# Query projection and output projection of a gated cross-attention kernel as three matmuls of high and low parts

## The reference

```python
# layer 1 (the code calls it L0): 16 heads of 16
q  = LN_head(LN(x) @ Wq)                 # per head layer norm of queries and keys
k, v = ctx @ Wkv
x  = x + tanh(g0) * (softmax(q k^T) v @ Wp + bp)      # Wp: the output projection of layer 1
x  = x + tanh(f0) * tanh(LN(x) @ W @ aux1 @ aux2 + b)
# layer 2 (L1): 8 heads of 64, keys from the tokens too
x  = x + tanh(g1) * (softmax(q1 [k1; k2]^T) [v1; v2] @ Wo + bo)
x  = x + tanh(f1) * mixture_of_8_experts(LN(x))       # the 2 best of 8 for each token
```

## Time and profile before

| | |
|---|---|
| median of 3 runs | 584.75 us (584.33 to 585.51) |
| the profiled execution, first to last instruction | 581.6 us |
| PE busy | 555.4 us, 95% |
| weight loads (PEld), beside PE | 477.1 us, 82% |
| DVE busy | 408.8 us, 70% |
| ACT busy | 319.4 us, 55% |
| POOL busy | 271.9 us, 47% |
| layer 1's quads | about 19 to 202 us |

### The profile page before, as it was taken

How to read it: one execution, slowest core, us unless ns; L and a number is a source line. 1 busy time by engine, 2 the same in 40 slices (tenths; PEclk the granted TensorE clock), 3 DMA queues, 4 the chain that set the end, 5 groups by cost and what they waited for, 6 DMA issues and landing times.

```text
span 581.6 us, 13614 instructions
## 1 busy us (share of the span) xinstructions
PE 555.4 (95%) x5542; PEld 477.1 (82%) x5542; DVE 408.8 (70%) x831; ACT 319.4 (55%) x632; POOL 271.9 (47%) x237
## 2 busy tenths in 40 slices
PE   8999999999989999999999999998999999999994
PEld 8776667677657878888888888877899999979994
DVE  7877568578696666777767867767677677746652
ACT  3554555555664665566555556654465656636641
POOL 3755655765740164657567465731203233421424
PEclk9999999999999999999999999999999999999998
DMA  8910840000000000000000000019374567726112
GB/s 259 357 45 2 318 194 3 1 3 2 2 2 1 2 1 2 8 9 17 18 9 18 10 25 1 25 26 414 91 253 149 170 213 253 259 32 236 28 20 26
DMA packets 24091, 50.92 MB, mean 88 GB/s; under 512 B 7072, under 2 KB 17104, under 8 KB 20688
## 3 DMA queue, kind: packets, MB, share of 16 engines
q1 hardware_dynamic: 18560, 45.20, 21.4%
q0 software_dynamic: 4224, 3.70, 3.6%
q10 hardware_dynamic: 1232, 1.01, 0.6%
HBM read 37.89 MB, written 13.31 MB: 88 GB/s over the span
## 4 chain that ended last, share of the span: by engine, by line
PE 81%; DVE 7%; ACT 5%; POOL 4%; issue 2%; DMA 1%; POOLq 0%; DVEq 0%; ACTq 0%
PE ps L59 15%; PE ps L60 14%; PE ps L61 14%; PE ps L607 5%; PE ps L750 4%; PE ps L625 4%; PE ps L768 4%; PE ps L738 4%; ACT P L1642 3%; DVE KN L1140 3%; PE ps L641 3%; PE ps L515 2%; PE ps L816 2%; POOL P L1947 2%; PE ps L522 2%
## 5 line engine op out<-in xcount | busy, mean ns | idle before, releaser
L1947 POOL TENSOR_SCALAR P<-P,rinv 112x487 f32<-112x487 f32 x56 | 88.2, 1588 | 50.9 <-DVE rinv L1183 50.7
L1140 DVE TENSOR_REDUCE KN<-ps 112x4 f32<-112x1500 f32 x32 | 55.0, 1719 | 28.7 <-PE ps L607 28.6
L424 POOL DMA_INDIRECT out<-WS,rows_i x16 | 28.7, 1791 | 92.5 <-ACT WS L1789 89.0
L60 PE MATMUL ps<-XGf,WH 128*128 128x256 f32 x252 | 71.3, 283 | 0.0
L61 PE MATMUL ps<-XGf,WL 128*128 128x256 f32 x252 | 71.3, 283 | 0.0
L59 PE MATMUL ps<-XGf,WH 128*128 128x256 f32 x252 | 71.3, 283 | 0.0
L1886 POOL TENSOR_TENSOR sr<-sv,mhalf 125x32 f32<-125x32 f32 x13 | 70.7, 5435 | 1.1
L1521 DVE TENSOR_TENSOR WL<-WR,WH 128x1024 fp32r<-128x1024 f32 x48 | 57.1, 1219 | 13.6 <-ACT WH L1843 10.0
L1642 ACT ACTIVATE P<-ps 125x1344 f32<-125x1344 f32 x32 | 41.3, 1292 | 32.8 <-PE ps L625 32.8
L1705 ACT ACTIVATE P<-ps,nm 112x487 f32<-112x487 f32 x64 | 41.9, 664 | 31.7 <-DVE nm L1175 31.7
L1843 ACT ACTIVATE WH<-WR 128x1024 fp32r<-128x1024 f32 x48 | 48.7, 1049 | 0.1
(11 more groups left out here) (290 smaller groups left out, 1546.1 us busy)
## 6 DMA issues: line engine op xcount, KB each, us to landing
WR<-in_gupT SPq DMA_DIRECT2D x16, 1024.0 KB, 7.2
WR<-in_dwnT SPq DMA_DIRECT2D x8, 1024.0 KB, 10.3
xs<-ZT SPq DMA_DIRECT2D x14, 516.0 KB, 6.0
CT<-in_ctxT SPq DMA_DIRECT2D x1, 2250.0 KB, 11.1
P<-xs SPq DMA_DIRECT2D x7, 256.0 KB, 10.8
P<-xs SPq DMA_DIRECT2D x9, 128.0 KB, 2.6
Wk<-in_L_xattn_Wk SPq DMA_DIRECT2D x2, 512.0 KB, 11.1
Wv<-in_L_xattn_Wv SPq DMA_DIRECT2D x2, 512.0 KB, 11.1
```

Source lines behind the costliest of these rows:

```text
L60: e.matmul(out, ah, bl, start=False, stop=False)
L1140: e.tensor_reduce(heads(KN[b % 2][0:NQ, 3, :])[:, 4 * k:4 * k + 4, 16], ps[0:NQ, 0:4, 0:NC], AX.X, ALU.max, negate=True).then_inc(s("smax" ...
L1947: e.tensor_scalar(P[:, k, 0:487], P[:, k, 0:487], rinv[:, k:k + 1], None, ALU.mult).then_inc(s("psc"), 1)
```

## The change

Two projections of layer 1 are computed by `matmul3` in place of float32 matmuls: the query projection of batches 3 to 7 (`QUERY_SPLIT = 3`), and the output projection of all 8 batches.

- The weights `Wp` and `Wq0` are split once, by new steps `wd 0` and `wd 1`: the high part on ACT (128x512), the low part on DVE (128x512).
- For batches 3 to 7, `xtc b 0` writes the high part of the turned tokens, and a new step `xtl b 0` on DVE computes the low part (128x224). It reads PSUM too, so that the bank of `xt b 0` is read out by `xtl`, no longer by `xtc`.
- `aT` of layer 1 writes the high part, and a new step `aTl` on DVE the low part (128x224). The bank of `awT` is read out by `aTl`.
- `WO` is loaded by SP after the eighth `wo` and behind the DMAs from `ZT`, no longer at the start. Its place in SBUF now holds `DH`, the high parts of `Wp` and `Wq0`, until then.

```diff
+QUERY_SPLIT = 3
...
+def has_low(b, r):
+
+    return r == 0 and b >= QUERY_SPLIT
...
+    if stage == "xt" and has_low(*i):
+        return ("xtl", *i)
+    if stage == "awT":
+        return ("aTl", *i)
...
-PREP = ((-38.14, "cs"), (-46.29, "norm", 0), (-31.45, "kp", 1, 0), (-31.42, "xt", 0), (-31.79, "xtc", 0),
+PREP = ((-38.14, "cs"), (-46.29, "norm", 0), (-31.45, "kp", 1, 0), (-31.42, "xt", 0), (-31.79, "xtc", 0), (-31.2, "xtl", 0),
...
                         for sem_, v in emptied(("xt", b, 0)):
                             w.wait_ge(sem_, v)
+                        if b >= QUERY_SPLIT:
+                            w.wait_ge(s("wd"), dense_split(1))
                         for k in range(2):
-                            t = e.matmul(ps[0:NQ, bk, 256:512], XT[:, k, b * NQ:(b + 1) * NQ], Wq0[:, k, :],
-                                         start=(k == 0), stop=(k == 1))
+                            if b < QUERY_SPLIT:
+                                t = e.matmul(ps[0:NQ, bk, 256:512], XT[:, k, b * NQ:(b + 1) * NQ], Wq0[:, k, :],
+                                             start=(k == 0), stop=(k == 1))
+                            else:
+                                t = matmul3(e, ps[0:NQ, bk, 256:512], tokens(b, k), [W_[:, k, :] for W_ in Wqs],
+                                            k == 0, k == 1)
...
+                        elif n < NB:
+                            t = matmul3(e, ps[0:NQ, bk, 0:256], [a[:, g * NQ:(g + 1) * NQ] for a in aT0],
+                                        [W_[:, g, :] for W_ in Wps], g == 0, g == nt - 1)
...
+                elif stage == "xtl":
+                    b, r = i
+                    w.wait_ge(s("xth"), high_order.index((b, r)) + 1)
+                    if b > QUERY_SPLIT:
+                        w.wait_ge(s("kp"), o_("kq", b - 1, 0))
+                    e.tensor_tensor(XTl, ps[:, bank("xt", b, r), 0:2 * NQ].rearrange("p (k n) -> p k n", k=2),
+                                    f_(XTh[:, :, b * NQ:(b + 1) * NQ]), ALU.subtract).then_inc(bank_sem("xt", b, r), 1)
+                elif stage == "aTl":
+                    n, = i
+                    if n:
+                        w.wait_ge(s("wo"), n)
+                    w.wait_ge(s("aT0"), n + 1)
+                    e.tensor_tensor(aT0[1], ps[:, bank("awT", n), 0:2 * NQ], f_(aT0[0]),
+                                    ALU.subtract).then_inc(bank_sem("awT", n), 1)
+                elif stage == "wd":
+                    k, = i
+                    w.wait_ge(s("wda"), dense_split(k))
...
+                    (high, low), W = ((Wps, Wp), (Wqs, Wq0))[k]
+                    e.tensor_tensor(low, W, f_(high), ALU.subtract).then_inc(s("wd"), 1)
...
-            e.dma_start(WO, pk("L1_xattn_Wo")).then_inc(s("in_WO"), 16)
...
+            w.wait_ge(s("wo"), NB)
+            e.dma_start(WO, A["L1_xattn_Wo"].rearrange("(k p) n -> p k n", p=128)).then_inc(s("in_WO"), 16)
```

More of the change, by code:

```diff
@@ L115 @@
 VALUES_1 = ((-15.23, "v", 1, 0), (-15.6, "vc", 1), (0.74, "v", 0, 0), (3.95, "v", 0, 1), (5.45, "vc", 0))
-TAIL0 = ((27.84, "ob"), (30.99, "obT"), (31.7, "aw"), (33.53, "awT"), (34.16, "aT"), (45.83, "wo"),
+TAIL0 = ((27.84, "ob"), (30.99, "obT"), (31.7, "aw"), (33.53, "awT"), (34.16, "aT"), (34.9, "aTl"), (45.83, "wo"),
          (47.46, "res", 1), (58.84, "stats", 1), (64.34, "norm", 1), (71.13, "xt", 1), (72.21, "xtc", 1),
@@ L191, in attention_order @@
         for d, stage, *i in (PREP if b >= 2 else ()) + (VALUES if b >= 2 else VALUES_1 if b else ()) + TAIL0:
-            at(t + d, stage, b, *i)
+            if stage != "xtl" or has_low(b, *i):
+                at(t + d, stage, b, *i)
     for d, stage in FFW:
@@ L352, in build @@
         FW = [cols(2048 + 512 * i, 2, 256) for i in range(3)]
+        XTh = XTo[:, :].rearrange("p (a b) -> p a b", a=2)
+        XTl = tile("XTl", 128, 2, NQ)
+        Wqs, Wps = ([t.rearrange("p (a b) -> p a b", a=2) for t in (B["DH"][:, 512 * k:512 * k + 512], XGf[:, o:o + 512])]
+                    for k, o in enumerate((0, 1536)))
         GW = sb("GW", [128, 2, NE])
@@ L527, in context0, with tokens, dense_split @@
             return t
+        def tokens(b, k):
+            return XTh[:, k, b * NQ:(b + 1) * NQ], XTl[:, k, :]
+        dense_order = [x[1] for x in order.entries if x[0] == "wd"]
+        def dense_split(k):
+            return dense_order.index(k) + 1
+        high_order = [x[1:] for x in order.entries if x[0] == "xtc" and has_low(*x[1:])]
         def tensor_attention(e, w):
@@ L801, in tensor_attention @@
                     bk = take(stage, n)
-                    nt, W = (2, Wp) if n < NB else (4, WO)
-                    w.wait_ge(s("in_Wp" if n < NB else "in_WO"), 16)
+                    nt = 2 if n < NB else 4
+                    if n >= NB:
+                        w.wait_ge(s("in_WO"), 16)
                     if n < NB:
+                        w.wait_ge(s("wd"), dense_split(0))
                         for sem_, v in emptied(("awT", n)):
@@ L1071, in vector_attention @@
                                     ALU.subtract).then_inc(s("cs"), 1)
+                elif stage == "xtl":
[15 more added lines that the diff above has]
+                    w.wait_ge(s("wda"), dense_split(k))
+                    if k:
+                        for b in range(QUERY_SPLIT):
+                            w.wait_ge(s("kp"), o_("kq", b, 0))
+                    (high, low), W = ((Wps, Wp), (Wqs, Wq0))[k]
+                    e.tensor_tensor(low, W, f_(high), ALU.subtract).then_inc(s("wd"), 1)
                 elif stage == "xs1":
@@ L1542, in scalar_attention @@
                     w.wait_ge(s("xt"), o_("xt", b, r))
-                    e.activation(XT[:, :, b * NQ:(b + 1) * NQ],
+                    low = has_low(b, r)
+                    e.activation((XTh if low else XT)[:, :, b * NQ:(b + 1) * NQ],
                                  ps[:, bank("xt", b, r), 0:2 * NQ].rearrange("p (k n) -> p k n", k=2),
-                                 ACT.Copy).then_inc(bank_sem("xt", b, r), 1)
+                                 ACT.Copy).then_inc(s("xth") if low else bank_sem("xt", b, r), 1)
                     if r == 3:
@@ L1650, in scalar_attention @@
                                  ACT.Copy).then_inc(bank_sem(src), 1)
+                elif stage == "wd":
+                    k, = i
+                    if k:
+                        w.wait_ge(s("dve0"), Q_SET)
+                    else:
+                        w.wait_ge(s("in_Wp"), 16)
+                    high, W = ((Wps[0], Wp), (Wqs[0], Wq0))[k]
+                    e.activation(high, W, ACT.Copy).then_inc(s("wda"), 1)
                 elif stage == "k1c":
@@ L1720, in scalar_attention @@
                         w.wait_ge(s("awT"), n + 1)
-                        e.activation(aT[:, 0:2 * NQ], ps[:, bank("awT", n), 0:2 * NQ], ACT.Copy).then_inc(
-                            bank_sem("awT", n), 1)
+                        e.activation(aT0[0], ps[:, bank("awT", n), 0:2 * NQ], ACT.Copy).then_inc(s("aT0"), 1)
                     else:
```

11 lines of the change are left out of this document (6 added, 5 removed).

## The result

| | before | after |
|---|---|---|
| median | 584.68 us (584.33 to 585.51, 4 runs) | 590.25 us (589.56 to 590.59, 4 runs) |
| span of the profiled execution | 581.6 us | 588.1 us |
| mean granted clock in it | 0.995 | 0.994 |

The changed kernel takes 1.0099 times as long, 95% interval 1.0087 to 1.0111: 5.6 us slower, where 4.1 were forecast.

A forecast was written before the change was run, and what follows sets the result against it. The prediction took TensorE, busy for 95% of the span, as the bound, in a closed ring with ScalarE and VectorE. Stalls 5.7 less matmuls 1.5 gave +4.1 on 581.6, plus 3.15: 588.8 us, range 586.2 to 590.9.

The forecast's parts named there:

- The stall: TensorE waits at `spq` for `xtl` to free the shared bank: 1.04 us in batches 4 to 7, 1.5 in batch 3.
- the 0.6 to 0.9 that the prediction asked for: Sign: layer 1's batch period of about 22 us grows by 0.6 to 0.9 us, the stall less the two projections.
- Nothing absorbed: Layer 1: delaying `st` delays `ex` and the next `S0` equally, so waits before `S0` don't shrink; 5.7 us lost.
- The rival of full absorption: Waits before `S0` shrink by as much as `spq` is late; only the 1.5 us gain remains: 583.2 us, chance 0.05.
- that of half of it: Waits in layer 1 take up 2.8 of the 5.7 us lost: +1.3, 586.1 us, chance 0.09.
- The matmuls: Layer 1's 13 projections as three matmuls: 8 save 0.16 us each, 5 save 0.05 each, 1.5 us gained.
- The four passes of the Trainium skill's page: Float32 matmuls make four passes, so each projection saves 2 passes, 0.21 us; 2.8 us over 13.
- the rival built on it: Projections pay no changeover between matmul kinds and gain 2.8 to 3.1 us: 587.4 us, chance 0.09.
- `aTl` costs nothing: VectorE's `aTl` runs while TensorE stands, its bank is read out in time; 0.35 us per batch if cover fails.
- The load: `WO`, issued after `wo 7` at about 226 us, takes 6 us, lands at 233, before ScalarE wants it at 236.66.
- The sum: Whole kernel: 5.7 - 1.5 = +4.1 us against the 581.6 us span, giving 585.7, or 588.8 us as median.
- The 3.15 us between span and median: Whole kernel: the median of 584.75 us lies 3.15 us outside the 581.6 us span; this distance was kept.

The follow-up runs named there:

- reads_only: The changed kernel with all its new steps, banks and places, but both projections as float32 matmuls again; 589.99 us, ratio 1.0095 to the kernel before.
- out_only: The changed kernel with only the output projection as three matmuls, query projection float32, no `xtl`, no `wd 1`; 586.63 us, ratio 1.0038 to the kernel before.
- query_only: The changed kernel with only the query projection of batches 3 to 7 as three matmuls, no `aTl`, no `wd 0`; 583.59 us, ratio 0.9985 to the kernel before.
- after_warm: The changed kernel with 28 in place of 18 idle transposes at 408 us; 587.71 us, ratio 1.0059 to the kernel before.
- before_warm: The kernel before with 28 in place of 18 idle transposes at 408 us; 583.39 us, ratio 0.9987 to the kernel before.
- after_again: The changed kernel run once more, with nothing altered; 589.08 us, ratio 1.0079 to the kernel before.

## Why the prediction was right, and where it was off

**The stall: right.** Forecast 1.04 us in each of batches 4 to 7 and 1.5 in batch 3, 5.7 in all; measured 1.09 to 1.10 and 1.34, 5.7 in all. In batch 4 `spq` itself is 1.04 us later behind `xt`, and the other 0.06 us lie between `spq` and `st`, 0.53 us apart where it was 0.47. A batch's period grew by 0.79 us, within the 0.6 to 0.9 that the prediction asked for. In batch 3 VectorE does what was written down, `max0` late, `wd 1`, `xtl`:

```profile
55.64 1.71 DVE L1202 TENSOR_REDUCE KN<-ps 112x4 f32<-112x1500 f32 x1
57.27 0.68 DVE L1133 TENSOR_TENSOR XGf<-WS,DH 128x512 fp32r<-128x512 f32 x1
57.87 0.38 DVE L1117 TENSOR_TENSOR XTl<-ps,XTo 128x224 fp32r<-128x224 f32 x1
```

The total of 5.7 us came out because two errors cancel, 4 x 0.05 us too little and 0.16 too much. The 0.16 us less in batch 3 come from `max0`, late by 0.37 us and not 0.44 (the start's 0.53 taken off), and from `wd 1`, 0.60 us to the next step and not 0.69.

**Nothing absorbed: right.** The waits before `S0` are 6.2 us before and after, and in `reads_only` too. The rival of full absorption is out, and that of half of it.

**The matmuls: mis-sized, 1.9 us and not 1.5.** Eight projections were 0.155 us each, as forecast (0.16). The five behind a float32 step were put at 0.05 us, because the first float32r matmul there costs 0.23 us from start to start and not 0.12. Timeline of the kernel after, batch 5, which answers to the earlier trace rows:

```profile
108.90 0.36 PE L573 MATMUL ps<-ident,XN 112*128 112x112 f32 x2
109.03 0.35 PE L59 MATMUL ps<-DH,XTo 128*112 128x256 f32 x1
109.22 0.28 PE L60 MATMUL ps<-XGf,XTo 128*112 128x256 f32 x1
...
109.90 0.92 PE L660 MATMUL ps<-QB,KT 32*125 32x112 f32 x24
```

The first matmul costs 0.19 us, 0.07 more than the next ones. But it starts 0.13 us behind the transposes, where the float32 projection started 0.20 us behind them, so the changeover is paid only once in either kernel. Transposes and projection together took 1.15 us and take 1.00. The prediction measured the projection from its own first record and left out what lies ahead of it. Batch 7's output projection saved 0.08 us. In all 12 x 0.155 + 0.08 = 1.9 us, and `reads_only` shows the same once its earlier start is taken off. The four passes of the Trainium skill's page that the prediction names would have given 0.21 us each; no run shows that, and the rival built on it (2.8 to 3.1 us) is out.

**"`aTl` costs nothing": wrong, 0.5 us.** In batch 5 it pushes the maximum of quad 27 back by 0.21 us. In batch 7 it waits for ScalarE, and a copy of layer 2's probabilities waits behind it:

```profile
218.53 0.61 DVE L1410 COPY P<-ps 125x448 f32<-125x448 f32 x1
219.68 0.39 DVE L1124 TENSOR_TENSOR HTf<-ps,HTf 128x224 fp32r<-128x224 f32 x1 [0.54 <-ACT HTf L1792]
219.99 0.57 DVE L1301 SCALAR_TENSOR_TENSOR X<-tt,tg,X 112x256 f32<-112x256 f32 x1
220.49 0.61 DVE L1410 COPY P<-ps 125x448 f32<-125x448 f32 x1
```

The prediction had looked for cover in batches 4 to 7's preparation and not where the last batches' tail lies beside layer 2. It did name the price, 0.35 us, and this is what it cost at 218 us. `out_only` shows the same two losses (0.20 and 0.38 us), `query_only` neither.

**The load: right**, though 3.3 us and not 6.

**The sum.** 5.7 - 1.9 + 0.5 = 4.3 us. In `after_warm`, whose profiled execution has no drop of the clock, the distance to the kernel before grows by 4.5 us from the first quads (-0.34) to the end of layer 2 (+4.1). Its median is 4.3 us over that of `before_warm`. The forecast of 4.1 is that, with two errors of 0.4 and 0.5 us that cancel. What is beyond is the clock: 0.5 us against a kernel that meets the drop in half of its executions, which makes 4.8, and `after_again` measured 4.99. The first measurement, 5.57, is 0.6 us more; the transposes of the start, late by 0.53 us in its profiled execution through the clock, take 5.5 to 7.1 us among the profiled executions of all these kernels, and the kernel without the change's arithmetic was later still.

One step was put wrongly and did no harm. The 3.15 us between span and median aren't time outside the span. In each execution whose span is known that distance is 1.7 to 1.9 us. So the profiled execution of before took some 583.4 us, 1.3 us less than the median, and the forecast against the median was right only because the difference of like with like was carried over.

## What to carry to other kernels

When a change adds a reader to a buffer that is handed out by a rule, look first at who gets the buffer next: here three fifths of the stalls came from a bank that moved, with nothing to do with the work added, and one number in a table took back half of it. A second read behind the first puts a round trip over two engines between two neighbouring instructions of the engine that bounds the kernel (1.09 us), seven times what one cheaper projection gave. And price a replaced instruction from the start of the step ahead to the start of the step behind, so that a changeover isn't counted twice.

## What the runs showed of the hardware

- After waits of 1.27 and 0.5 us, the granted clock fell to the lower level for most of a stretch of 4.5 us, in some executions of a kernel and not in others. It cost 1.1 us in the traces, 0.7 to 1.2 between the groups of executions. With ten more idle transposes in the wait none of 14 executions of two kernels showed it by the mean clock; without them 8 of 8 and about half did. In a third kernel with the ten transposes 5 of 12 executions had the lower mean clock.
- The first transposes of a program follow each other every 0.21 us and then every 0.11 us, and the change comes after 13 to 28 of them from one profiled execution to another. That alone makes starts differ by up to 1.6 us, of which 1.1 us are left at layer 1's first quad.
- Behind a float32 transpose, the first float32r matmul costs 0.07 us more than the next (0.19 against 0.12 us), and it starts 0.07 us sooner behind the transposes than a float32 one did.
- GpSimd's power on 125x32 elements took 5.43 to 5.46 us in all 14 traces, but for one place in three executions of two kernels that share an order of TensorE's steps, 7.66 to 7.67 us. Its cause is open.
- VectorE's 125x512 multiplication took 1.21 us and not 0.68 us when GpSimd's 112x256 multiplication started 0.06 to 0.07 us ahead of it, and ended 0.56 us after that one. The Trainium skill, "Trainium Architecture — The Big Picture", What this means for kernel authors, names a port that these two share and lock; the rows agree.
